# Bringing expert rows back by plain row runs and a matrix of ones, in a fused GNN and mixture-of-experts kernel

## The reference

```python
# layer 1, on x normalised by row
agg = segment_sum(feat[src], dst);  deg = segment_sum(1, dst)
x = x + feat @ W_self + (agg / max(deg, 1)) @ W_neigh + b
# layer 2, on x normalised by row: 8 experts, each node goes to its best two
logits = xn @ Wr + br;  w = softmax(top-2 logits)
y = sum over the two experts e:  w_e * (gelu(xn @ W1[e] + b1[e]) @ W2[e] + b2[e])      # 256 -> 512 -> 256
x = x + y
```

## Time and profile before

| | us |
|---|---|
| median of 3 runs | 1268.87 (1264.01 to 1272.49) |
| the profiled execution | 1265.15 |
| its span, first to last instruction | 1263.1 |
| granted TensorE clock, mean over the span | 0.969 of full speed |
| busy: PE, DVE, POOL, ACT | 1095.5, 865.6, 942.5, 435.7 |

### The profile page before, as it was taken

The page is one execution under the profiler, slowest core; times in us unless marked ns, Lnnn a source line. Parts: engine busy times, 40 slices in busy tenths (PEclk is TensorE's granted clock), DMA queues, the critical chain, the costliest instruction groups (busy, mean ns, idle before and its releaser), DMA issues.

```text
span 1263.1 us, 22169 instructions
## 1 busy us (share of the span) xinstructions
PE 1095.5 (87%) x6356; PEld 971.6 (77%) x6357; DVE 865.6 (69%) x2812; ACT 435.7 (34%) x812; POOL 942.5 (75%) x980
## 2 busy tenths in 40 slices
PE   0479999989987999999899898987989887988987
PEld 0368888979976888998788787776778776877977
DVE  7886766777676767768767675855667764655447
ACT  7723322323433334434434443433224312211131
POOL 7677777777667777777777777777777777777774
PEclk9999999999998999999999898998999999999989
DMA  9999987866556476666756665656687668766766
GB/s 351 328 317 377 301 294 262 287 199 211 179 166 202 146 253 198 221 199 207 213 183 199 187 191 185 195 162 209 188 259 221 211 213 275 227 219 210 230 206 227
DMA packets 163993, 287.57 MB, mean 228 GB/s; under 512 B 25632, under 2 KB 93344, under 8 KB 163744
## 3 DMA queue, kind: packets, MB, share of 16 engines
q1 hardware_dynamic: 115280, 153.36, 36.5%
q0 software_dynamic: 45696, 124.88, 32.6%
q10 hardware_dynamic: 2896, 7.87, 1.7%
HBM read 228.81 MB, written 57.20 MB: 226 GB/s over the span
## 4 chain that ended last, share of the span: by engine, by line
PE 54%; POOL 13%; DVE 12%; issue 9%; DMA 7%; SPq 2%; ACT 1%; DVEq 0%; POOLq 0%; ACTq 0%
PE bank L966 17%; PE bank L1042 13%; POOL ring L689 11%; PE bank L1068 8%; PE bank L1076 5%; PE bank L995 3%; PE bank L954 3%; PE bank L997 2%; DMA ring<-feature_table,src_sb 2%; DMA heap<-in_x 1%; PE bank L1092 1%; DVE heap L1480 1%; POOL pair L711 1%; DVE agg L1323 1%; PE bank L1103 1%
## 5 line engine op out<-in xcount | busy, mean ns | idle before, releaser
L689 POOL DMA_INDIRECT ring<-feature_table,src_sb x756 | 743.1, 983 | 248.1 <-issue 218.9
L966 PE MATMUL bank<-ring,onehot 128*128 128x257 f32 x1544 | 393.3, 399 | 100.0 <-issue 57.9
L966 PEld LDWEIGHTS bank<-ring,onehot 128*128 128x128 f32 x1544 | 302.0, 199 | 157.9 <-issue 109.9
L868 ACT ACTIVATE heap<-heap 128x512 f32<-128x512 f32 x139 | 87.8, 632 | 335.2 <-DVE heap L1480 335.2
L1480 DVE TENSOR_TENSOR heap<-bank,b_sb 128x512 f32<-128x512 f32 x139 | 95.9, 690 | 145.0 <-PE bank L1042 77.4
L1068 PE MATMUL bank<-heap 128*128 x728 | 182.5, 395 | 13.7 <-DVE y_out L1489 7.9
L1042 PE MATMUL bank<-row_t,heap 128*128 128x128 f32 x1456 | 179.1, 277 | 0.7 <-DVE heap L1480 0.6
L1042 PEld LDWEIGHTS bank<-row_t,heap 128*128 128x128 f32 x1456 | 173.4, 194 | 2.6 <-issue 1.1
L1068 PEld LDWEIGHTS bank<-heap 128*128 128x128 f32 x728 | 137.2, 196 | 31.8 <-issue 14.7
L1323 DVE SCALAR_TENSOR_TENSOR agg<-bank,in_first,agg 128x257 f32 x196 | 94.4, 482 | 96.5 <-PE bank L966 62.9
L1281 DVE TENSOR_TENSOR onehot<-iota,target 128x512 f32<-128x512 f32 x196 | 134.2, 685 | 7.1 <-DVE xf L1340 4.8
(11 more groups left out here) (193 smaller groups left out, 1250.6 us busy)
## 6 DMA issues: line engine op xcount, KB each, us to landing
heap<-in_w SPq DMA_DIRECT2D x139, 512.0 KB, 5.0
expert_out<-empty_row SPq DMA_DIRECT2D x68, 256.0 KB
ring<-feature_table,src_sb POOLq DMA_INDIRECT x756
row<-expert_rows SPq DMA_DIRECT2D x91, 128.5 KB, 4.3
xf<-in_x SPq DMA_DIRECT2D x49, 128.0 KB
ff<-feature_table SPq DMA_DIRECT2D x49, 128.0 KB
expert_out<-inside SPq DMA_DIRECT2D x46, 128.0 KB
expert_out<-y_out SPq DMA_DIRECT2D x45, 128.0 KB
```

What stands on the lines that cost most here:

```text
L689: pool.indirect_dma_start(group_row(t, i)[:, 0:D], None, x if t < RAW else table, bass.IndirectOffsetOnAxis(src_sb[:, k:k + 1], 0)).then_i ...
L868: act.activation(hid[s], hid[s], ACT.Gelu).then_inc(S.gelu, 1)
L966: last = pe.matmul(bank[t % 2][:, 0:D + 1], onehot[:, q, i, :], group_row(t, i), start=(i == 0), stop=(i == GT - 1))
```

## The change

- POOL's two indirect DMAs of each merge within the loop are gone. There are 25 such merges now (blocks 1 to 28 without the dense ones), in the slots 143 to 191.
- In their place SP reads, in the merge's slot, one plain run of 64 rows from each expert's section of `expert_out`, from the place where this block's rows begin (`fetch_runs`, eight DMAs at addresses read from `starts`). Each row now carries a tag, its node's number + 1, in a 257th column. In the next slot DVE turns the tags of the 512 rows into four 128x128 matrices of ones and zeros (`hot_runs`); one slot on PE multiplies them with the rows in `result_b` (`sum_runs`), DVE adds the sum to x1 (`add_runs`), and one slot later SP stores x1 (`store_added`).
- There is one buffer for the runs, and `sum_runs` shares `result_b` with the units.
- Before a fetch, SP waits until all tiles stored so far have landed; before the next tile's store it waits until the runs have landed.
- Block 18 is routed, not dense: 93 tiles and 40 early dense units in place of 91 and 48.
- Of the 18 merges behind the loop the first 12 need 89 of the 93 tiles stored, and none starts before the last group is summed.
- The tag costs one small DVE instruction for each routed block and one for each tile; the claims check the length of the runs (64 at most) as well.

```diff
-DENSE_BLOCKS = (0, 3, 6, 9, 18, 47)
+DENSE_BLOCKS = (0, 3, 6, 9, 47)
+UNCLAIMED = 4
+RUN = 64
-    for tiles, upto in (*claimed, (lists[-1][1] - NE, LAST_CLAIM), (lists[-1][1], NB - 3)):
+    for tiles, upto in (*claimed, (lists[-1][1] - UNCLAIMED, LAST_CLAIM), (lists[-1][1], NB - 3)):
-                merges.append((m, tiles, at if tiles < lists[-1][1] - NE and at < NG else None))
+                merges.append((m, tiles, at if tiles <= lists[-2][1] and at < NG else None))
-    R = D + 1
+    R = D + 2
+    Y = D + 1
+            def fetch_runs(i):
+                n, tiles, at = merges[i]
+                if i:
+                    sp.wait_ge(runs_sum, X_IN + i)
+                sp.wait_ge(main.rows_set, rank[n] + 1)
+                tiles_put(hold, main, tiles_stored[0])
+                for e0 in range(0, NE, 4):
+                    firsts = load_values(mybir.EngineType.SP, starts[0:1, i, e0:e0 + 4], NE * CAP, **unchecked)
+                    for e, first in enumerate(firsts, e0):
+                        p0, h = e * RUN % P, e * RUN // P
+                        sp.dma_start(runs_in[p0:p0 + RUN, h, :], expert_out[bass.ds(first, RUN), :]).then_inc(runs_landed, 16)
+            def store_added(i):
+                sp.wait_ge(runs_added, X_IN + i + 1)
+                sp.dma_start(nodes(out, NB - 1 - merges[i][0]), x1_of(main, merges[i][0])).then_inc(d_out, 16)
 # store_rows
+                if S.planned and runs_fetched[0]:
+                    sp.wait_ge(runs_landed, X_IN + 16 * NE * runs_fetched[0])
 # SP, slot t: the tile's store, then
-                for i in merges_in(t, -1):
-                    store_merged(i)
+                for i in merges_in(t):
+                    fetch_runs(i)
+                for i in merges_in(t, -3):
+                    store_added(i)
 # POOL, take_rows
-                if k >= STAGE_BUFFERS:
-                    pool.wait_ge(summed, NG)
-                else:
+                pool.wait_ge(summed, NG)
+                if k < STAGE_BUFFERS:
+                    pool.wait_ge(runs_sum, X_IN + STAGE_MERGES)
 # POOL, slot t
-                for i in merges_in(t):
-                    take_rows(i)
 # PE: results and early_result
+                    if runs_summed[0]:
+                        pe.wait_ge(runs_added, X_IN + runs_summed[0])
+            def sum_runs(i):
+                pe.wait_ge(runs_landed, X_IN + 16 * NE * (i + 1))
+                pe.wait_ge(runs_hot, X_IN + i + 1)
+                result_free(units_done[0])
+                if i:
+                    pe.wait_ge(runs_added, X_IN + i)
+                halves = NE * RUN // P
+                for h in range(halves):
+                    last = pe.matmul(result_b[:, 0:D], run_hot[:, h, :], runs_in[:, h, 0:D], start=(h == 0), stop=(h == halves - 1))
+                last.then_inc(runs_sum, 1)
 # PE, slot t: turns, hidden, count, place, router, turn_normal, product, then
+                for i in merges_in(t, -2):
+                    sum_runs(i)
 # (results of the slot's unit and the group follow)
 # DVE
+            def hot_runs(i):
+                dve.wait_ge(runs_landed, X_IN + 16 * NE * (i + 1))
+                if i:
+                    dve.wait_ge(runs_sum, X_IN + i)
+                link(dve.tensor_scalar(tags[:, :], runs_in[:, :, D], float(-P * merges[i][0] - 1), None, ALU.add))
+                dve.tensor_tensor(run_hot, iota[:, :].unsqueeze(1).broadcast_to([P, halves, P]),
+                                  tags[:, :].unsqueeze(2).broadcast_to([P, halves, P]), ALU.is_equal).then_inc(runs_hot, 1)
+            def add_runs(i):
+                dve.wait_ge(runs_sum, X_IN + i + 1)
+                dve.tensor_tensor(x1, x1, result_b[:, 0:D], ALU.add).then_inc(runs_added, 1)
 # slots
+                if S.planned and rank[n] <= STAGE_MERGES:
+                    dve.tensor_copy(starts[0:1, rank[n], :], places[0:1, :])
+                if S.planned:
+                    dve.tensor_scalar(rows[s][:, :, D + 1], iota_p[:, 0:1].broadcast_to([P, 2]), float(P * n + 1), None, ALU.add)
 # weighted
+                dve.tensor_copy(y[:, D:Y], row[S.slot(j, XR)][:, D + 1:R])
```

More of the change, by code:

```diff
@@ L165, in build @@
     STAGE_MERGES = len([at for n, tiles, at in merges if at is not None])
-    merge_buffer = [i % STAGE_BUFFERS if i < STAGE_MERGES else (i - STAGE_MERGES) % MERGE_BUFFERS for i in range(len(merges))]
+    merge_buffer = [None if i < STAGE_MERGES else (i - STAGE_MERGES) % MERGE_BUFFERS for i in range(len(merges))]
     merge_use = [merge_buffer[:i].count(merge_buffer[i]) for i in range(len(merges))]
@@ new lines, in build @@
+        pairs = sb("pairs", [P, 2 * (STAGE_BUFFERS - 1) * Y])
+        pair = [pairs[:, 2 * k * Y:2 * (k + 1) * Y] for k in range(STAGE_BUFFERS - 1)]
+        runs_in = pairs[:, :].rearrange("p (h y) -> p h y", y=Y)
+        assert 2 * (STAGE_BUFFERS - 1) * P == NE * RUN and P % RUN == 0
+        starts = base_i[0:1, 0:(STAGE_MERGES + 1) * NE].rearrange("o (k e) -> o k e", e=NE)
+        assert (STAGE_MERGES + 1) * NE <= NG + 3 * NE - 4 and all(rank[merges[i][0]] == i for i in range(STAGE_MERGES))
@@ new lines, in build @@
+        ring_flat = ring[:, :, :].rearrange("p a b -> p (a b)")
+        merge_b = [dst_i[:, DK * P:DK * P + 2 * Y].bitcast(F32), *pair]
+        merge_b += [ring_flat[:, k * 2 * Y:(k + 1) * 2 * Y] for k in range(GS * GT * (D + 1) // (2 * Y))]
+        merge_b += [onehot_flat[:, k * 2 * Y:(k + 1) * 2 * Y] for k in range(GS * GT * P // (2 * Y))]
+        merge_b += [target[:, 0:2 * Y]]
+        assert len(merge_b) == MERGE_BUFFERS
+        run_hot = merge_b[0][:, 0:NE * RUN].rearrange("p (h t) -> p h t", t=P)
@@ L320, in build @@
+        y_out = [inside[:, s * Y:(s + 1) * Y] for s in range(in_scratch)] + [sb(f"y_out{s}", [P, Y]) for s in range(in_scratch, XY)]
         small_in, dst_in, src_in, w2_in = (sem(n) for n in ("small_in", "dst_in", "src_in", "w2_in"))
@@ L1599, in _, with unit_sums @@
                     x1_sums(main, n)
-                for u in early_in(t, "sum"):
-                    if u % NE == 0:
-                        dense_shares(DENSE_BLOCKS[u // NE], 3 * (u // NE))
-                    if DENSE_BLOCKS[u // NE] == LAST - 1:
-                        dve.wait_ge(added, t - 1)
-                    early_sum(u)
-                for j in tiles_in(t, "weigh"):
-                    weighted(main, j, of_tile.pop(j))
+                def unit_sums(now):
+                    for u in early_in(t, "sum"):
+                        if (dense_at["result"][u] == t) == now:
+                            if u % NE == 0:
+                                dense_shares(DENSE_BLOCKS[u // NE], 3 * (u // NE))
+                            if DENSE_BLOCKS[u // NE] == LAST - 1:
+                                dve.wait_ge(added, t - 1)
+                            early_sum(u)
+                    for j in tiles_in(t, "weigh"):
+                        if (tile_at["result"][j] == t) == now:
+                            weighted(main, j, of_tile.pop(j))
+                unit_sums(False)
+                for i in merges_in(t, -2):
+                    add_runs(i)
+                unit_sums(True)
                 if 1 <= t < NG:
@@ L1611, in _ @@
                     degrees(main, n, NB - 1 - n)
-                for i in merges_in(t):
-                    add_rows(i)
+                for i in merges_in(t, -1):
+                    hot_runs(i)
             for i in range(STAGE_MERGES + sum(MERGES_BESIDE), len(merges)):
```

91 lines of the change are left out of this document (54 added, 37 removed).

## The result

The changed kernel takes 1384.71 us (median of four runs, 1382.21 to 1387.84) against 1266.44 (1260.91 to 1272.49): a ratio of 1.0934 [1.0875, 1.0993]. The direction was forecast; the size was not. 1308 us had been predicted, and the range ended at 1332.

What follows compares the result with a forecast made beforehand. POOL's gathers were taken to set the pace, with PE close behind. From 1265.15 us, +41.6 for slots 144 to 195, -2.5 for the earlier start and +4 for the tail gave 1308 us; range 1262 to 1332.

Steps and rivals of the forecast that it cites:

- What bounds the kernel: Slots 144 to 195: POOL's gathers set the pace, PE close behind; nearly all of POOL's 60 us is hidden behind PE.
- Block 18: Stretch 440 to 560 us: eight dense units leave PE, two tiles come; gain nothing, cost 2.5 us for POOL's two scatters.
- PE in the slots 144 to 195: PE's work there, nothing waited for, grows from 288 to 336.8 us, a floor 7.0 us under the 343.8 of before.
- not slower: Rival: DVE's add is hidden and PE runs without pause at its floor, 336.8 us; 1260 us whole; chance 0.12.
- The bank: PE's results behind a sum wait for DVE's add_runs, about 0.9 us for each of 24 sums, 21.6 us.
- DVE at nothing: DVE's tags, one-hots and addition replace a merge's additions at no cost; without room it would be 10 us.
- SP, the new work: SP's loop of fetch issues, landings, stores and loads takes 14.9 us per two slots, against PE's 14.3.
- PE paces: Rival: SP keeps up, slots 144 to 195 last 368.4 us, +24.6; 1291 us whole; chance 0.31.
- The sum: Slots 144 to 195: cycles, ends, block loads and close_lists together 385.4 us against 343.8, +41.6.
- The start and early stage: Slot 144 begins 2.5 us earlier, two merges gone before it; longer rows' DMA volume costs nothing; equal to 830 us within 3.
- The clock: PE's clock in the stage, at 0.97 of full speed, could give back up to 10 us with gather waits gone.
- SP far behind: Rival: landings at their medians and above, SP loops of 16 to 18 us, 1335 us and more; chance 0.11.

## Why the prediction was wrong

**Where the stage's 452 us go**, each from two kernels above:

| | us | from |
|---|---|---|
| the kernel before without its merges in the loop | 315 | its own row |
| a tile and a half, tags, adds, one DMA, one quarter of the sums, lower clock | 31 | 346 - 315 |
| the other three quarters of the sums (and the one-hots, which alone were worth nothing) | 27 | 373 - 346 |
| the shared bank | 28 | 401 - 373 |
| the fetch's eight issues, ahead of the loads and tied to the sum | 51 | 452 - 401 |

Before pays 30 over the 315 (345), and the change 137. The removed cost was half of what POOL's issue time (60 us) says, and of its replacements the sums, the bank and SP's issues all lie on PE's path; only DVE's one-hots don't.

**What bounds the kernel: right.** POOL's 60 us were mostly hidden behind PE: taking them away entirely gains 34 us, 30 of them in this stage.

**Block 18: right**, nothing gained. Its 2.5 us of cost stand in the prediction's text but are missing from its sum, which would have been 1311 with them.

**PE in the slots 144 to 195: the floor was too low.** It counted 288 us of work in before by start-to-start prices, and 336.8 after. PE is busy for 306.0 in the row of that stage. The added 48.8 were right: 306.0 + 48.8 = 354.8, and the kernel with one DMA from the still array shows 354.82 (that the two agree to the digit is luck; in the changed kernel, at a clock of 0.94, it is 370.5). The error, 18, is in the 288, which was never held against the busy time of the same stretch. The overlap of spans isn't it: the busy time of a stretch counts overlapping spans once (the three rows of PE from 1099.96 to 1105.20 add up to 5.74 us, and the stretch shows 5.24), so it may be compared with start-to-start prices. About six of the 18 are the clock, by an estimate (288 / 0.98 = 294); where the rest lies, no experiment took apart. The block work, rounded to 3.0 each, is the least certain of the prices. With 306 in place of 288 the floor after the change lies 10 us above the 345 of before, so at the clock of these runs (0.97 in that kernel) hiding all waits would not have made the forecast's third case, not slower.

**The bank: right in size.** 21.6 predicted, 27.5 waited (23 times), 28 when removed. But it counts in full only without SP's loop: alone it gave nothing, and with the loads first 14.

**DVE at nothing: right** for the matrices of ones, by the run without them. The tags were not tested.

**SP, the new work: wrong, and the main error.** The step said that w1 and the row load are "hidden behind the landing of the runs" and that landings close the loop, 14.9 us a cycle. On the issues it was right: 5.4 to 6.2 us a fetch. On the landings it was off both ways: 2.14 for the runs in the cycle shown, where 3.2 was taken, and 5.02 for the store, where 3.0 was. The Trainium skill ("DMA: Bandwidth & Descriptors", Anatomy of one DMA) gives a transfer some 2.0 us and its bytes over 436 GB/s, by an estimate from it about 2.3 for a tile; its fit is of DMAs issued by GpSimd, and these are SP's. The medians, 4.1 for stores and 4.9 for rows, are about twice that; the measurement decides. Yet SP's waits for landings weren't the point, since with all of them taken away the stage stays at 451. What failed is the structure: the loads of the coming tile are issued behind the fetch, the fetch waits for the sum, and the next sum stands on PE behind the turn and hidden matmuls which need those loads. The prediction had both halves in one sentence ("whichever of the two is late in a cycle delays both") and priced neither: it took the larger of SP's 14.9 and PE's 14.3, where the two lie partly in series. The cycle is 17.8, and all 24 of them take 428 us where the prediction had 351 (13 at 14.9 and 11 at 14.3). Of the stage, the step gave 17 us over the "PE paces" case (385.4 - 368.4); it is 51. By cutting it in three ways (loads first -23, second buffer -34, one issue and no landing waits -51) the runs show it.

**The sum**, then: +41.6 forecast for the stage, 107 measured. The 66 missing are, as far as differences between kernels may be added, 18 of floor, 6 of bank, 34 of SP's loop, and some 8 of PE's other waits: 19 in the kernel with one DMA (401 - 354.8 - 27.2) where 10 were carried over from before.

**The start and early stage: wrong.** -2.5 forecast; +10 measured. By the gathers, 12 us are lost before slot 50 (289.7 to 301.7) and 4 won back from there to slot 143 (563.9 to 559.9), in which stood the first two merges of before. "DMA volume by a few MB: nothing" was the step. Between 48 us and slot 50, the queue's packets, MB and share of 16 engines, and the w1 loads' time to landing, before (48 to 290 us) and after (48 to 302):

```profile
q1 hardware_dynamic: 39422, 45.53, 57.9%
...
heap<-in_w SPq DMA_DIRECT2D x29, 512.0 KB, 5.7
```
```profile
q1 hardware_dynamic: 39434, 45.62, 64.2%
...
heap<-in_w SPq DMA_DIRECT2D x29, 512.0 KB, 8.9
```

The same packets and bytes take 16% more time on the DMA engines (0.642 x 254 = 163 against 0.579 x 242 = 140 us of each), and w1 lands 3.2 us later. What differs is the rows' length, 1028 and 1032 bytes for 1024 and 1028. The Trainium skill (the same page, How a descriptor splits into AXI transactions) says that where a piece doesn't start on a 256-byte boundary, its first transaction starts at the boundary below it, and the bytes ahead of the start are fetched, not used, and still cost. The rows agree in direction with this; no run here varies the alignment alone.

The other kernels bear out the added DMA time, but not that it makes slot 50 late. In the twelve changed kernels with small pieces the queue's time up to slot 50 is 154 to 166 us, in the kernel before without its merges 140. In the two with large pieces it is 139 and 140 (25,816 packets in place of 39,434), and yet slot 50 begins there at 294.1 and about 294, no earlier than at 292.7 in the kernel with two buffers, whose queue takes 154. Over all kernels slot 50 begins at 288.3 to 293.6 in the three of the old form and at 292.7 to 301.7 in the changed ones. So the early stage is longer by some 7 us in the middle of these ranges; what makes it so, and how much of the 12 us between the two profiles is spread between executions, stays open.

**The tail: right.** +4 forecast within 0 to 9, +2 measured.

**The clock: wrong in sign.** Up to 10 us back was thought possible; it fell from 0.98 to 0.94 in the stage. The long waits for rows are not all of the cause: the kernel with one matmul in four waits only 2.6 us for rows there and has 0.94 too.

**The rivals.** "SP far behind" had the right culprit at 0.11, and its price, 1335 and more, was still 50 short: it rested on longer landings, in 13 of the 24 cycles. At its own 16 to 18 us for all 24 the stage would have grown by 33 to 81 over the forecast, where it was given 20 to 35. "Not slower" needed the pauses behind the sums to be under 0.3 us; even without them the floor is 354.8, above the 345 of before. Of the signs that were named, fetches came 16.7 us apart and the row waits appeared, as for SP pacing; but SP also waited in them for the sum (35.5 us), which was named as the sign that PE paces. Both at once is what the loop through the two looks like. The runs landed in under 2.5 us in the cycle shown, a named sign of being wrong, and it wasn't this that made it wrong.

## What to carry to other kernels

An engine's busy time that runs beside another engine's is worth only what the run without it gives; here 60 us were worth 34, and that single measurement (or a floor of PE's work that is held against the busy time of the same stretch) bounds the whole idea. When a step puts several us of issues into a queue, list what is issued behind it, follow that to the engine that waits, and see whether the step's own condition stands behind that wait: then the pieces add up, and the larger of two loops is no longer the answer. A shared bank is priced only after the pacing wait is gone; here, removing it before that just moved the wait (0 us alone, 28 at the end).

## What the runs showed of the hardware

- After PE had stood still from 1190.89 to 1195.89, its 16 hidden half-passes took 3.28 us, against 1.95 at 1185.48 in the same cycle. The granted clock by stretches (last three columns: clock, DMA share, GB/s):

```profile
1168.00:1190.00 22.00, 21.12 (x121) 18.70 (x122) 11.63 (x29) 3.51 (x7) 11.30 (x12) 1.00 0.59 172
...
1196.00:1200.00 4.00, 4.00 (x21) 3.95 (x22) 0.13 (x1) 0.81 (x2) 0.16 (x1) 0.60 0.76 198
1200.00:1204.00 4.00, 3.40 (x16) 2.69 (x15) 1.38 (x3) 0.63 (x1) 0.00 (x0) 1.00 0.11 30
```

  A mean of 0.60 of 2.4 GHz over those 4 us is mostly the lower level, 1.2 GHz, and then full speed again. So a 5 us wait for a row cost 1.3 us more in matmuls. The kernel with the longest such waits (60.9 us, up to 10.7) had the lowest clock in the stage, 0.91; but 0.94 came with 36.1 us of them and with 2.6, so they are not the only cause.
- Eight 64 KB DMAs with addresses from memory held SP for 5.39 and 6.16 us in the two fetches shown, the first two DMAs 0.65 apart, while the last of them landed 2.14 us after its issue began: the issues, not the transfer, were the long part.
- Rows four bytes longer, at equal packets and bytes, went with 16% more DMA time up to slot 50 (10 to 19% in the twelve changed kernels that cleared with small pieces); with the clearing in pieces of 4112 bytes the excess was gone (139 us against 140).
